# One exchange on ScalarE in a two-layer gated attention and expert kernel: a unit's exponentials and the copy of half of the next unit's values

## The chip, the cores and the metric

The kernel runs on one core of one Trainium2 chip. The metric is the device time of one execution in microseconds (us).

## What is computed

32 sequences of 128 tokens with 128 features pass through two layers. Each layer adds a cross attention over 77 context rows per sequence, scaled by tanh of a gate, and then a mixture of 8 experts of which each token takes 2, scaled by a second gate. Only the attention of layer 0 (8 heads of 64) is touched by the change. Cut to that:

```python
q = (x @ Wq).reshape(B, N, 8, 64).transpose(0, 2, 1, 3)        # x: layernormed
k = (context @ Wk).reshape(B, M, 8, 64).transpose(0, 2, 1, 3)
v = (context @ Wv).reshape(B, M, 8, 64).transpose(0, 2, 1, 3)
attn = jax.nn.softmax(jnp.einsum('bhnd,bhmd->bhnm', q, k) * scale, axis=-1)
out = jnp.einsum('bhnm,bhmd->bhnd', attn, v)
x = x + jnp.tanh(g_xattn[0]) * (out.transpose(0, 2, 1, 3).reshape(B, N, 512) @ Wo + bo)
```

## The kernel before

All engines walk the same list of units of work, the plan; each engine picks the kinds that concern it and issues its part in the order of the list. Waits are on semaphores only, so an engine that waits holds back everything behind it on that engine. `order()` writes the list out from four phases: layer 0's attention, layer 0's experts, layer 1's attention, layer 1's experts, each overlapping the next by a few steps. `attention0_steps` gives one step for each unit u, a unit being one sequence of 128 tokens with all 8 heads over its 77 keys (616 columns).

The query and key weights are multiplied into one matrix per head beforehand, and so are the value and output weights. Float32 products are made of three passes over a high and a low part. For unit u the pieces are:

- **score0** (PE, L840, six products into two banks): needs the normalised rows of the group of four sequences, their keys, and that DVE has subtracted the row maxima of unit u-1, since there is one pair of score banks. DVE then reduces the row maxima (L1265, row_max) and subtracts them (L1268, into prob).
- **exp0** (ACT, L1151): the exponentials, in place in prob. **divide0**: DVE sums the rows (L1319, row_sum) and takes the reciprocal (L1322); POOL multiplies (L1615).
- **turn0** (PE, L863, transposes in two sets, copied by ACT, L1171), one step later; **weigh0** (PE, L881, the product with the values in five chunks; DVE adds the gated result to x_res, L1328), two steps later.
- **v0** of unit u+1, in two halves of four heads (PE, L776 to L778, 77 x 512; copied by ACT, L1156, from bank to the tile vo). Both halves use one bank, so PE begins half 1 when ACT has copied half 0. SP sends each half out to DRAM (L690), and v0_load brings the rows back in the order of weigh0's chunks (L696, L697). ACT's copies of a unit wait until the halves of the unit before have landed in DRAM.

Between these lie the preparations for later groups, dealt out by u mod 4 in `prepare_attention0_at`: the key blocks of the next group (k0: PE L776 to L778 at 128 x 308; ACT copies the high part, L1113; DVE takes the difference as the low part, L1281), its norm, normalisation and transposition (xt). The bank of such a product is free again when DVE has taken the low part, and two banks alternate; one of them is the routing's too. `route_tasks` puts the routing of finished groups into the steps from unit 6 on (mturn L975, route L983 and L1378, pick L1396 to L1417, rank L999 and L1424, scatter L1687 on POOL).

`u` in the rows below: unit 16 is at about 141 to 145 us, unit 19 at 161 to 167, unit 21 at 174 to 180, unit 22 at 180 to 187.

Of the kernel before, what the change touches and what calls it, by code (L numbers as in the profile page):

```python
# [30 lines left out]
NSEQ, SEQ, D, NKEY = 32, 128, 128, 77  # L31
# [94 lines left out]
def attention0_steps(tasks):  # L126
    background = [("ctx", i) for i in range(2, CTX_SETS)] + [("weights1",), ("tables", 0)]
    background += [("expert", 0, e) for e in range(NEXP)] + [("tables", 1)]
    for u in range(NSEQ + 4):
        step = []  # L130
        more = prepare_attention0_at(u) if u < NSEQ else ([], [], [], [])
        if u < NSEQ:
            step += [("score0", u)] + more[0] + [("exp0", u)]
        if 0 <= u - 2 < NSEQ:
            step.append(("weigh0", u - 2))
        if u < NSEQ:
            step += [("v0_load", u)] + [("v0", u + 1, 0)][:u + 1 < NSEQ] + [("divide0", u)] + more[1]
        if 0 <= u - 1 < NSEQ:
            step.append(("turn0", u - 1))
        if u < NSEQ:  # L140
            step += [("v0", u + 1, 1)][:u + 1 < NSEQ] + [("bias0", u)] + more[2]
        step += more[3] + tasks.get(u, [])
        if background:
            step.append(background.pop(0))
        if u == NSEQ - 1:
            step += [("fetch", i) for i in range(AHEAD)]
        yield step
# [51 lines left out]
def prepare_attention0_at(u):  # L199

    g = (u + 1) // GS + 1 if u >= GS - 1 else 1
    if g >= NG:
        return [], [], [], []
    keys = ((3, 2, 1, 2) if g > 1 else (3, 3, 2, 0))
    turn = u % GS
    before = sum(keys[i] for i in ((3, 0, 1, 2) if g > 1 else (0, 1, 2))[:(turn + 1) % GS if g > 1 else turn])
    places = [[("k0", g, before + n)] for n in range(keys[turn])]
    if turn == 2:
        places.append([("xt", g)])
    places += [[]] * (3 - len(places))  # L210
    return places + [[("norm", g)] if turn == 0 else [("normalize", g)] if turn == 1 else []]
# [82 lines left out]
def order():  # L294

    first = prepare_attention0(0)
    out = [first[0], ("turn_weight", 0), ("turn_weight", 1), ("ctx", 0), ("wqk", 0), ("wqk", 1), ("turn_weight", 2)]
    out += first[1:] + [("wvo", 0), ("wvo", 1), ("ctx", 1), ("v0", 0, 0), ("v0", 0, 1), ("gates",)]
    tasks = [route_tasks(0, GS, 6, ((range(7), (5, 6, 7, 8)), (range(7), (5, 6, 7, 8)), ((0, 1, 2, 3, 3, 4, 5), (5, 5, 5, 5)))),
             route_tasks(1, 2 * GS, 13, (((0, 1, 3, 5, 6, 7, 9), (9, 11, 13, 15)), ((0, 1, 3, 5, 6, 7, 9), (8, 9, 10, 11)),  # L300
                                         ((0, 1, 2, 3, 4, 5, 6), (6, 6, 7, 7))))]
    after0 = [[("expert", 1, e)] for e in range(NEXP)] + first_keys_and_queries()
    phases = [(attention0_steps(tasks[0]), NSEQ), (expert_steps(0, tasks[0], NSEQ + 4, after0), LAYER_BLOCKS + 2),
              (attention1_steps(tasks[1]), U1 + 1), (expert_steps(1, tasks[1], U1 + 5, []), LAYER_BLOCKS)]
    begun = 0
    for i, (phase, alone) in enumerate(phases):
        after = phases[i + 1][0] if i + 1 < len(phases) else iter(())
        for _ in range(alone - begun):
            out += next(phase)
        begun = 0  # L310
        for step in phase:
            out += step
            out += next(after, [])
            begun += 1
        if i + 1 < len(phases):
            out += next(after)
            begun += 1
    out += [("spread", n) for n in ON_PE] + [("keep_busy",)] + [("load_last", q) for q in range(HT // 2)]
    out += [("combine_last", n) for n in range(HT)]
    apart = {t[1:] for t in out if t[0] == "rest"}  # L320
    return [u for t in out for u in ([t, ("rest",) + t] if t[0] in SPLIT_KINDS and t not in apart else [t])]
# [1402 lines left out]
```

## Time and profile before

| | |
|---|---|
| median of 3 runs | 786.98 us (784.69 to 788.65) |
| profiled execution | 788.87 us |
| its span in the trace | 787.1 us |
| mean granted TensorE clock | 0.928 of full speed |
| busy over the span | PE 85%, DVE 73%, POOL 60%, ACT 57% |

The span is what the profiler saw of one execution, from its first to its last instruction; what lies around it is 1.8 us here. Engines: PE is TensorE (PEld its weight loads), DVE VectorE, ACT ScalarE, POOL GpSimd, SP SyncE. Busy time is that of instructions, without waits. A granted clock of 1.00 is 2.4 GHz, of 0.50 it is 1.2 GHz, and a number between is the mean of a stretch with both.

### The profile page before, as it was taken

What the parts mean: (1) busy time and instruction counts of PE and PEld (TensorE: products, weight loads), DVE (VectorE), ACT (ScalarE), POOL (GpSimd) and SP (SyncE); (2) the same over time, 40 slices, a digit from 0 to 9 for tenths busy, and PEclk for the clock granted to TensorE, in tenths of its full rate; (3) what the DMA queues carried; (4) which work ended last, traced back from release to release, by engine and by line L of the source; (5) the groups of instructions that cost most, each with busy time, mean ns of one, the idle gap of its engine ahead of it and who ended that gap; (6) DMA issues with size and microseconds to landing.
All of it is one profiled execution on the core that took longest, in us unless ns stands there. A gap on an engine that the chain in (4) does not pass through costs nothing.

```text
span 787.1 us, 17248 instructions
## 1 busy us (share of the span) xinstructions
PE 672.4 (85%) x4720; PEld 609.5 (77%) x4720; DVE 574.3 (73%) x2005; ACT 448.7 (57%) x1219; POOL 475.7 (60%) x693
## 2 busy tenths in 40 slices
PE   6888988988887889988979898899888886878896
PEld 5667887877776889987878787788887886877796
DVE  3467877788667587999896888988878753845772
ACT  3466755665454555766666776676576543434451
POOL 4035346667457777787463344676566567677771
PEclk9999989998789799999998999999899986999998
DMA  9637546434344234545633534433534013344645
GB/s 263 176 82 191 161 136 172 120 112 128 102 113 131 86 102 115 151 117 143 174 87 90 118 90 90 129 100 76 119 93 99 24 43 96 107 120 122 188 132 178
DMA packets 130990, 95.91 MB, mean 122 GB/s; under 512 B 30504, under 2 KB 119112, under 8 KB 130832
## 3 DMA queue, kind: packets, MB, share of 16 engines
q1 hardware_dynamic: 113200, 69.15, 33.5%
q0 software_dynamic: 9088, 19.68, 7.7%
q10 hardware_dynamic: 8608, 5.99, 2.7%
q8 instruction: 40, 0.66, 0.4%
q14 instruction: 54, 0.44, 0.2%
HBM read 55.09 MB, written 44.10 MB: 126 GB/s over the span
## 4 chain that ended last, share of the span: by engine, by line
PE 40%; DVE 26%; issue 10%; ACT 9%; DMA 6%; POOL 5%; SPq 1%; DVEq 1%; ACTq 0%; POOLq 0%
PE banks L1032 9%; PE banks L896 4%; PE banks L1051 4%; DVE row_max L1265 4%; DMA y_rows<-y_sb,result_at 3%; DVE prob L1268 3%; PE banks L776 3%; PE banks L881 2%; PE banks L778 2%; PE banks L777 2%; PE banks L840 2%; POOL x_rows L1687 2%; ACT vo L1156 2%; POOL y_rows L1694 2%; PE banks L863 2%
## 5 line engine op out<-in xcount | busy, mean ns | idle before, releaser
L1694 POOL DMA_INDIRECT y_rows<-y_sb,result_at x156 | 151.0, 968 | 57.0 <-issue 30.2
L1032 PE MATMUL banks<-xb,up 128*128 128x128 f32 x936 | 143.5, 293 | 15.9 <-DVE hidden L1513 5.0
L1687 POOL DMA_INDIRECT x_rows<-xm,row x128 | 127.6, 997 | 36.0 <-issue 30.2
L1032 PEld LDWEIGHTS banks<-xb,up 128*128 128x128 f32 x936 | 125.9, 204 | 22.3 <-issue 10.1
L1051 PE MATMUL banks<-down,hidden 128*128 x624 | 100.4, 285 | 9.3 <-DVE y_sb L1530 8.7
L1649 POOL TENSOR_TENSOR v_flat<-v_raw,row_head 104x64 f32<-104x64 f32 (+1 forms) x128 | 55.7, 464 | 74.3 <-ACT v_raw L1187 73.9
L1051 PEld LDWEIGHTS banks<-down,hidden 128*128 128x128 f32 x624 | 85.5, 198 | 12.5 <-issue 12.1
L896 PE MATMUL banks<-v_flat,prob_t 128*128 128x108 f32 (+2 forms) x640 | 88.7, 288 | 3.2 <-issue 1.6
L896 PEld LDWEIGHTS banks<-v_flat,prob_t 128*128 128x128 f32 (+1 forms) x640 | 81.9, 202 | 11.0 <-ACT prob_t L1171 6.2
L1265 DVE TENSOR_REDUCE row_max<-banks 128x8 f32<-128x616 f32 x96 | 75.6, 787 | 20.4 <-PE banks L840 11.9
L1171 ACT ACTIVATE prob_t<-banks 128x512 f32<-128x512 f32 x192 | 72.6, 432 | 28.1 <-PE banks L863 26.2
L1615 POOL TENSOR_TENSOR prob<-prob,inv_sum 128x616 f32<-128x616 f32 x32 | 38.9, 1217 | 67.1 <-DVE inv_sum L1322 67.1
L1225 ACT ACTIVATE gate<-banks,block_bias 128x128 f32<-128x128 f32 x156 | 48.8, 364 | 45.0 <-PE banks L1032 40.5
L1505 DVE COPY up<-up 128x256 f32 x156 | 57.4, 368 | 11.0 <-issue 4.2
L1229 ACT ACTIVATE hidden<-banks 128x256 f32<-128x256 f32 x78 | 29.9, 384 | 60.1 <-PE banks L1032 56.4
L1268 DVE TENSOR_TENSOR prob<-banks,row_max 128x616 f32<-128x616 f32 x75 | 60.0, 800 | 2.6
L863 PE MATMUL banks<-ident,prob 128*128 128x128 f32 (+1 forms) x375 | 55.6, 281 | 0.0
L1513 DVE SCALAR_TENSOR_TENSOR hidden<-banks,block_bias,gate 128x128 f32<-128x128 f32 x156 | 46.9, 341 | 10.1 <-ACT gate L1225 9.1
L776 PE MATMUL banks<-wvo_h,ctx_th 128*77 128x512 f32 x64 | 31.5, 492 | 25.4 <-ACT vo L1156 25.2
L881 PE MATMUL banks<-vo_flat,prob_t 128*128 128x128 f32 (+1 forms) x320 | 47.2, 302 | 3.4 <-ACT prob_t L1171 3.4
L1530 DVE COPY y_sb<-banks 128x128 f32<-128x128 f32 x78 | 22.4, 288 | 35.8 <-DMA y_rows<-y_sb,result_at 23.6
L881 PEld LDWEIGHTS banks<-vo_flat,prob_t 128*128 128x128 f32 (+1 forms) x320 | 45.6, 218 | 3.4 <-ACT prob_t L1171 3.4
(212 smaller groups left out, 1619.8 us busy)
## 6 DMA issues: line engine op xcount, KB each, us to landing
v_rows<-vo SPq DMA_DIRECT2D x64, 154.0 KB
vo_flat<-v_rows SPq DMA_DIRECT2D x32, 256.0 KB
x_norm<-x_rows SPq DMA_DIRECT2D x86, 72.0 KB
x_far<-x_rows SPq DMA_DIRECT2D x70, 72.0 KB
gathered<-y_rows ACTq DMA_DIRECT2D x32, 128.0 KB
q_rows<-up_raw SPq DMA_DIRECT2D x8, 512.0 KB, 2.8
q_even<-q_rows SPq DMA_DIRECT2D x12, 256.0 KB
q_odd<-q_rows SPq DMA_DIRECT2D x12, 256.0 KB
```

Of the source, the lines that this page charges most:

```text
L863: done = pe.transpose(banks[0:chunk_rows[c], PT_BANK[k], c % 4 * SEQ:(c % 4 + 1) * SEQ], flat[:, c * P:c * P + chunk_rows[c]], ident[:, :])
L881: done = pe.matmul(banks[:, O_BANK, 0:D], prob_t[0:rows, b % 2, c, :], vo_flat[0:rows, b % 2, c, :], start=c == 0, stop=c == CHUNKS - 1)
L896: done = pe.matmul(banks[:, O_BANK, half * width:half * width + cols], prob_t[0:rows, u % 2, c, :], v1_flat[0:rows, first:first + cols], s ...
L1032: done = pe.matmul(banks[:, UP_BANK[i % 2], part * P:(part + 1) * P], block_w[:, i % WR, part // 2, part % 2 * P:(part % 2 + 1) * P], xb[: ...
L1051: done = pe.matmul(banks[:, Y_BANK[i % 2], 0:D], hidden[:, i % HR, half, :], of_expert(flat[:, (2 * layer + half) * D:], i, D), start=half ...
L1171: act.activation(dst, banks[0:rows, PT_BANK[k], 0:len(chunks) * SEQ], ACT.Copy).then_inc(sem("prob_t"))
L1265: dve.tensor_reduce(m_view, s_view, AX.X, ALU.max).then_inc(sem("row_max"))
L1268: dve.tensor_tensor(prob_view.rearrange("p (k s) n -> p k s n", k=2), s_view, m_view.unsqueeze(3).to_broadcast([P, 2, 4, NKEY]), ALU.subtr ...
L1505: dve.tensor_copy(block_w[:, i % WR, 1 - layer, :], src[:, bass.ds(at, HID1)]).then_inc(sem("block_w_dve"))
L1649: pool.tensor_tensor(v1_rows[0:rows, b % 2, half, chunks[0]:chunks[-1] + 1, :, 0:DK1], v1_raw[0:rows, chunks[0]:chunks[-1] + 1, half, :, : ...
L1687: pool.indirect_dma_start(out=x_rows[i // HG][:, :], out_offset=bass.IndirectOffsetOnAxis(ap=row[:, n, c:c + 1], axis=0), in_=xm[:, i % 2, ...
L1694: pool.indirect_dma_start(out=y_rows[k][:, :], out_offset=bass.IndirectOffsetOnAxis(ap=result_at[:, i % (2 * YR):i % (2 * YR) + 1], axis=0 ...
```

## The change

In each step of layer 0's attention the entry ("exp0", u) moves from before weigh0 to after ("v0", u + 1, 0). Only ACT does anything at exp0. It has nothing to do for weigh0 and v0_load, so on ACT the one effect is that exp0 of unit u comes after the copy of half 0 of unit u+1, and no longer before it. All other orders and all waits are as before.

```diff
@@ -130,11 +130,11 @@
         step = []
         more = prepare_attention0_at(u) if u < NSEQ else ([], [], [], [])
         if u < NSEQ:
-            step += [("score0", u)] + more[0] + [("exp0", u)]
+            step += [("score0", u)] + more[0]
         if 0 <= u - 2 < NSEQ:
             step.append(("weigh0", u - 2))
         if u < NSEQ:
-            step += [("v0_load", u)] + [("v0", u + 1, 0)][:u + 1 < NSEQ] + [("divide0", u)] + more[1]
+            step += [("v0_load", u)] + [("v0", u + 1, 0)][:u + 1 < NSEQ] + [("exp0", u), ("divide0", u)] + more[1]
         if 0 <= u - 1 < NSEQ:
             step.append(("turn0", u - 1))
         if u < NSEQ:
```

## Rows read from the trace of the kernel before

**Rows 1.** The page: busy time, share of the span and instructions of each engine.

```profile
PE 672.4 (85%) x4720; PEld 609.5 (77%) x4720; DVE 574.3 (73%) x2005; ACT 448.7 (57%) x1219; POOL 475.7 (60%) x693
```

**Rows 2.** Waits, 35 to 255 us: who waited for whom; us in total, times, longest.

```profile
ACT prob L1151 <- DVE prob L1268: 44.2, 27, 4.3
...
PE banks L776 <- ACT vo L1156: 24.6, 18, 3.0
...
DVE row_max L1265 <- PE banks L840: 11.9, 11, 4.0
DVE k_t L1281 <- ACT k_t L1113: 11.7, 15, 1.2
...
DVE rank_row L1424 <- PE banks L999: 5.0, 5, 1.4
...
ACT vo L1156 <- DMA v_rows<-vo: 3.9, 3, 2.8
...
DVE row_sum L1319 <- ACT prob L1151: 2.9, 6, 0.5
```

**Rows 3.** Timeline, unit 19: start us, us, engine line op out<-in xcount [idle before <-releaser].

```profile
161.42 0.40 PE L778 MATMUL banks<-wvo_l,ctx_th 128*77 128x512 f32 x1
...
162.80 0.80 DVE L1268 TENSOR_TENSOR prob<-banks,row_max 128x616 f32<-128x616 f32 x1
...
163.63 0.72 ACT L1151 ACTIVATE prob<-prob 128x616 f32<-128x616 f32 x1 [3.17 <-DVE prob L1268]
...
164.26 0.57 ACT L1156 ACTIVATE vo<-banks 77x512 f32<-77x512 f32 x1
...
164.88 0.46 PE L776 MATMUL banks<-wvo_h,ctx_th 128*77 128x512 f32 x1 [2.10 <-ACT vo L1156]
...
165.33 0.43 DVE L1281 TENSOR_TENSOR k_t<-banks,k_t 128x308 fp32r<-128x308 f32 x1
...
166.12 0.81 PE L840 MATMUL banks<-k_t,xt_h 128*128 128x308 f32 x4
166.30 0.19 DVE L1424 TENSOR_TENSOR rank_row<-banks,region 128x32 f32<-128x32 f32 x1 [0.54 <-PE banks L999]
```

**Rows 4.** Timeline, unit 21.

```profile
174.75 1.28 PE L881 MATMUL banks<-vo_flat,prob_t 128*128 128x128 f32 x10
...
175.36 0.80 DVE L1268 TENSOR_TENSOR prob<-banks,row_max 128x616 f32<-128x616 f32 x1
...
176.19 0.72 ACT L1151 ACTIVATE prob<-prob 128x616 f32<-128x616 f32 x1 [0.81 <-DVE prob L1268]
176.33 0.40 PE L778 MATMUL banks<-wvo_l,ctx_th 128*77 128x512 f32 x1
...
176.82 0.58 ACT L1156 ACTIVATE vo<-banks 77x512 f32<-77x512 f32 x1
...
176.95 0.80 DVE L1319 TENSOR_REDUCE row_sum<-prob 128x8 f32<-128x616 f32 x1
...
177.90 0.43 DVE L1281 TENSOR_TENSOR k_t<-banks,k_t 128x308 fp32r<-128x308 f32 x1
...
178.38 1.06 PE L983 MATMUL banks<-router,xm_t 128*128 128x8 f32 x8
```

**Rows 5.** Chain that ended last, unit 22: start us, us, what.

```profile
182.91 0.81 DVE row_sum L1319
...
188.40 0.81 DVE prob L1268
```

**Rows 6.** Timeline, unit 16.

```profile
141.83 2.01 PE L881 MATMUL banks<-vo_flat,prob_t 128*128 128x128 f32 x10
142.14 0.80 DVE L1268 TENSOR_TENSOR prob<-banks,row_max 128x616 f32<-128x616 f32 x1
...
144.15 0.40 PE L778 MATMUL banks<-wvo_l,ctx_th 128*77 128x512 f32 x1
```

**Rows 7.** Stretch 98 to 125 us: busy us (instructions), granted clock, DMA share, GB/s.

```profile
98.00:125.00 27.00, 23.71 (x145) 21.11 (x144) 20.71 (x74) 16.29 (x38) 12.74 (x18) 0.87 0.46 127
```

## The prediction

> **What bounds the kernel now.** I read the page's busy shares first: no engine is full over the span, PE 85%, DVE 73%, ACT 57% [rows 1]. The edit touches one stretch, layer 0's attention, about 35 to 255 us, so next come the waits of that stretch [rows 2]. Three rows decide. PE waits 24.6 us in 18 places for ACT's copy of the values (vo), nearly all of it before the second half of a unit's value product: both halves share one PSUM bank, so PE cannot write half 1 until ACT has copied half 0. ACT itself waits 44.2 us for DVE's subtraction before the exponentials. DVE waits little. So ACT is not short of time; it is short of order: it stands at the exponentials of unit u while the finished half 0 of unit u+1 lies behind them.
>
> The stretch is no single bound. It goes by fours, since the next group's keys, its norm, and the routing of an earlier group are dealt over u mod 4. The timelines of units 19 (u mod 4 = 3) and 21 (u mod 4 = 1) and the chain through unit 22 (u mod 4 = 2) show who is late.
> Unit 19 [rows 3]: half 0 is complete at 161.82 (161.42 + 0.40), the subtraction only at 163.60; the exponentials run 163.63 to 164.35, the copy starts at 164.26, and PE stands 2.10 us. DVE is late here.
> Unit 21 [rows 4]: the subtraction ends at 176.16, half 0 at 176.73. PE is late here, and ACT's exponentials fill just the gap; PE waits for nothing. Behind them on DVE lie the row sums (176.95), the reciprocal and the low half of a key block (177.90 to 178.33), and the router's product, which needs that block's bank, starts at 178.38.
> Unit 22 [rows 5]: the chain that ended last runs on DVE without a break from the row sums through the routing of a group to the next unit's subtraction (189.21).
>
> **The change, part by part.** Nothing is added or removed. On ACT, the exponentials of unit u (32 of them, 0.72 us [rows 3]) change places with the copy of half 0 of unit u+1 (0.57 to 0.58 us); 31 units have such a copy. PE, POOL and SP keep their orders; DVE too. The copy no longer waits for the subtraction; the exponentials now wait for half 0's product too, and for the copy's other wait, that the transfers of the previous unit's values out of that tile have landed. Behind the exponentials on ACT are the next key block's high half, the copies of the turned probabilities, and half 1's copy; who waits for them is DVE (row sums first), then PE and POOL.
>
> *Where DVE is late (u mod 4 = 3, and units 1, 2, 5, 25).* The copy moves from 164.26 to about 161.86, and PE's 2.10 us go. But the next scores also need the subtraction: PE may start them at 163.65 at the earliest, 2.5 before the 166.12 of [rows 3]. What comes next is DVE: after the subtraction its own work (low key block, residual, row sums, reciprocal, low key block) lasts to 165.76 as before, and what goes is its wait for the rank products, 0.54 us here. Over the stretch those waits are 5.0 us in 5 places [rows 2]; with 1.6 us of the 11.9 that row_max waits for PE (those in the same units) DVE gets at most 6.6 us back. So of PE's 24.6 us most turn into a wait for the scores' bank, which DVE's subtraction frees. Unit 25, where PE's wait is longest (3.0), gives 1.5: DVE has block tables to build there and the key copies before it are late too. Units 1 and 2 give 1.1: DVE waits there for ACT's high halves (that row of [rows 2]), and those come earlier only by the one copy of 0.57 that was passed. Unit 29 gives 0.5.
>
> *Where PE is late (17 units).* In unit 21 the copy would start at 176.77 instead of 176.82: it gains 0.05. The exponentials start 0.50 after it (0.59 less the 0.09 by which neighbours on ACT overlap, as 176.91 against 176.82), at 177.27 and not 176.19: 1.08 later. Row sums start at 178.01 and not 176.95, the low key block ends at 179.39 and the router's product starts 1.06 later, the scores behind it too. I give this full 1.06 to units 10, 13, 14, 21, 22 and 26: 6.4 us. In u mod 4 = 2 it is DVE's chain of [rows 5] that moves. In units 9, 17, 18 and 30 half 0 and the subtraction end together (within 0.15), so the exponentials lose only the copy: four times 0.59 less a little behind PE, 2.2. In units 3 to 8 DVE has little routing yet and part of row_max's 11.9 us of waits [rows 2] lies there; about a third of six times 1.06 stays: 2.4. Sum of losses 11.0.
>
> *Where PE is late because its clock is low (units 12, 16, 28).* The granted clock is 0.87 from 98 to 125 us [rows 7]; ten products of weigh0 take 2.01 us in unit 16 [rows 6], at the 1.2 GHz level, against 1.28 in unit 21 [rows 4]. Half 0 ends at 144.55, 1.61 after the subtraction (142.94). Here PE's earlier start from the unit before (about 2.5, as in unit 19) brings half 0 to about the subtraction, so the delay shrinks to the copy, and PE, which is behind everything, keeps what DVE cannot use: 2.6 us in the three. Behind units 20 and 24 ACT has four normalisations in line and gives 0.7 back.
>
> Sum: gains 6.6 + 1.5 + 1.1 + 0.5 + 2.6 - 0.7 = 11.6; losses 11.0; net 0.6 us sooner. Against the profiled execution's own 788.87 that is 788.3; its median of three is 786.98, so I say 786.4.
> After the stretch nothing changes but its offset: the experts and layer 1 start as early as this stretch ends.
>
> *Bounds.* The gain cannot exceed PE's removed waits, 24.6 us; nothing else gets shorter. The loss, if every late unit's 1.08 stayed and no wait came back, is 17 x 1.08 = 18.4. I take neither end: the scores need both PE's bank and DVE's subtraction, so each side limits the other.
>
> The Trainium skill (Perfetto Trace Analysis, Optimization Strategy) says to find the gaps of the most-contended engine and to make what they wait for come sooner. Followed here, with PE as that engine by its weight loads (77% of the span), the rule makes the time 24.6 us less; the row for DVE shows 5.0 of use to it. It is rival A below.
>
> **The rivals.**
> A, *PE's waits really go* (faster). For it: 18 waits, 24.6 us, and in the half-speed spells PE is behind all else. Against it: scores wait for the subtraction. If DVE keeps 6.6 and PE half of the remaining 18.0 while a third of the losses stay hidden behind PE, it is 6.6 + 9.0 - 7.3 = 8.3 less: 778.7. It decides when units with u mod 4 = 0 start at least 1 us earlier after their predecessor. By that rule of the skill it would be this mechanism in full, 762.4.
> B, *exponentials stand behind a copy whose product is late* (slower). DVE's row sums start 1.06 later in the 17 units and the chain of [rows 5] pays, while in u mod 4 = 3 only DVE's 5.0 come back: 11.0 - 5.0 = 6.0 more, 793.0. It decides when u mod 4 = 0 gives nothing back, as at full clock it might.
> C, *a transfer takes the wait's place*: ACT's copy waited 3.9 us in 3 places for values on their way out, once 2.8 [rows 2]; the exponentials now wait behind it. With the 1.2 us that the exchange itself costs in each, they come about 2 to 4 us late there, some 8 in all; 2.7 are in the sum above; with all on the chain it is 5.3 more than the forecast, 791.7.
> D, *the order does not matter*, because DVE binds throughout: 787.0.
>
> **How the numbers follow.** A measurement of this kernel tells a difference of 0.5%, 3.9 us, from none. The forecast (786.4) gets 0.40 and D 0.05, both within 0.5%; A 0.26; B 0.20; C 0.09. The forecast's own range is 783 to 790.5, since each of its two sums of 11 may be off by a quarter. For 8 in 10 the range goes to A's 778.7 less a little and B's 793.0 and more: 778 to 794. Faster by over 0.5%: 0.27; within: 0.45; slower: 0.28, of which all but little is B and C.
>
> **What would show it.** Right, if PE's wait for vo falls from 24.6 to under 5, if PE instead waits for DVE's subtraction (prob) before scores (none now), if DVE's wait for ACT's exponentials rises from under 3 to 15 or more, and rank_row's wait for PE falls from 5.0 to about 1. In a unit like 21 the row sums should follow the subtraction by about 1.85 us, not 0.79; in one like 19 the scores should follow it at once. The stretch from unit 0's row_max to unit 31's should be as long as now within 2 us. It is wrong if that stretch shrinks by over 4 (DVE had more slack than I gave it) or grows by over 4 (nothing is given back), or if PE's low-clock spells become fewer or more: at 1.2 GHz a unit's weigh0 costs 2.01 and not 1.28 us [rows 4, 6].

## The result, and the profile after

The changed kernel takes 792.01 us (median of 8 executions, 789.27 to 794.4), the kernel before 787.51 on the same chip (8 executions, 784.06 to 789.84): a ratio of 1.0076 with a 95% interval of 1.0052 to 1.0100, slower by about 6.0 us (4 to 8). Ratios, here and below, are those on record over fast executions alone and not the quotients of the medians; the two medians here are 4.5 us apart. The forecast was 786.4, no difference that can be told. The profiled execution has a span of 790.0 us, against 787.1.

The page of the kernel after, busy time and then the chain that ended last:

```profile
PE 667.2 (84%) x4720; PEld 600.9 (76%) x4720; DVE 578.5 (73%) x2005; ACT 445.2 (56%) x1219; POOL 475.5 (60%) x693
...
PE 33%; DVE 30%; issue 12%; ACT 11%; POOL 7%; DMA 4%; DVEq 1%; SPq 1%; POOLq 0%; ACTq 0%
```

The instruction counts are those of [rows 1]; PE's busy time is even 5.2 us less. On the whole span nothing points at the loss. So go to the stretch. From unit 0's row_max to unit 31's it lasts 218.29 us (35.64 to 253.93) and lasted 213.04 (35.55 to 248.59): 5.25 us more, in layer 0's attention. Behind it the changed kernel's span is 2.4 us shorter; the granted TensorE clock of the next 146 us was 0.97 there and 0.93 before. So the spans differ by only 2.9. The waits of the kernel after in this attention, 35 to 262 us (who waited for whom; us in total, times, longest):

```profile
DVE row_sum L1319 <- ACT prob L1151: 29.7, 26, 3.4
...
ACT vo L1156 <- PE banks L778: 25.0, 18, 3.0
...
ACT vo L1156 <- DMA v_rows<-vo: 18.3, 9, 3.0
ACT prob L1151 <- DVE prob L1268: 16.1, 9, 5.2
...
PE banks L996 <- DVE k_t L1281: 8.7, 4, 3.1
PE banks L776 <- ACT vo L1156: 8.3, 11, 2.6
DVE row_max L1265 <- PE banks L840: 8.0, 7, 4.0
ACT x_norm L1134 <- DVE shift_n L1307: 6.7, 7, 1.1
...
DVE rank_row L1424 <- PE banks L999: 2.8, 2, 1.4
...
PE banks L840 <- DVE prob L1268: 0.7, 1, 0.7
```

Against [rows 2] the reader sees both sides of the exchange. ACT's wait for the subtraction fell from 44.2 to 16.1 and PE's for vo from 24.6 to 8.3, 16.3 us that PE no longer stands there. In exchange DVE stands 29.7 us before its row sums (2.9 before), and there is a row that was not there at all: PE waits 8.7 us in 4 places to begin the rank products (L996), for DVE's low key block. ACT's normalisation waits 6.7 us for an instruction of DVE on four elements (shift_n), where it waited 1.3.

Where the 5.25 us lie: the step from one row_max to the next, after minus before, summed by the unit it starts from (worked out from the timelines of both). The forecast's column sorts the prediction's own terms by unit, with units 1 and 2 sharing their 1.1 and units 3 to 8 losing 0.4 each. The last column is a second trace of the changed kernel (the third group's, below) against the same trace of the kernel before; it shows how far single traces vary.

| step starts at | forecast | measured | second trace |
|---|---|---|---|
| u mod 4 = 1 | +1.1 | +1.6 | +1.1 |
| u mod 4 = 2 | +5.2 | +5.2 | +3.6 |
| u mod 4 = 3 | -5.8 | -0.4 | -0.4 |
| u mod 4 = 0 | -1.1 | -1.1 | -0.8 |

In three rows the sum came near the forecast; the gain in u mod 4 = 3 did not come in either trace.

**Where PE is late.** Timeline of the kernel after, units 21 and 22 (start us, us, engine line op, what [idle before <-releaser]); to be read beside [rows 4, 5]:

```profile
181.21 0.59 ACT L1156 ACTIVATE vo<-banks 77x512 f32<-77x512 f32 x1 [1.39 <-PE banks L778]
...
181.71 0.71 ACT L1151 ACTIVATE prob<-prob 128x616 f32<-128x616 f32 x1
...
182.45 0.79 DVE L1319 TENSOR_REDUCE row_sum<-prob 128x8 f32<-128x616 f32 x1 [1.20 <-ACT prob L1151]
...
183.39 0.42 DVE L1281 TENSOR_TENSOR k_t<-banks,k_t 128x308 fp32r<-128x308 f32 x1
183.56 1.22 POOL L1615 TENSOR_TENSOR prob<-prob,inv_sum 128x616 f32<-128x616 f32 x1 [0.57 <-DVE inv_sum L1322]
183.74 1.06 DVE L1307 SCALAR_TENSOR_TENSOR shift_n<-mean_var,rstd 128x4 f32<-128x4 f32 x1
183.87 1.06 PE L983 MATMUL banks<-router,xm_t 128*128 128x8 f32 x8 [1.03 <-DVE k_t L1281]
...
184.83 1.65 ACT L1134 ACTIVATE x_norm<-x_res,shift_n,rstd 128x128 f32<-128x128 f32 x4 [0.98 <-DVE shift_n L1307]
...
185.93 0.80 DVE L1265 TENSOR_REDUCE row_max<-banks 128x8 f32<-128x616 f32 x1
186.77 0.80 DVE L1268 TENSOR_TENSOR prob<-banks,row_max 128x616 f32<-128x616 f32 x1
...
188.66 0.71 ACT L1151 ACTIVATE prob<-prob 128x616 f32<-128x616 f32 x1
189.40 0.80 DVE L1319 TENSOR_REDUCE row_sum<-prob 128x8 f32<-128x616 f32 x1 [1.19 <-ACT prob L1151]
...
194.09 0.77 DVE L1265 TENSOR_REDUCE row_max<-banks 128x8 f32<-128x616 f32 x1
```

The exponentials start 0.50 behind the copy, as worked out, and DVE stands 1.20 us before the row sums. The router's product (L983) starts 4.90 us behind unit 21's row_max (178.97) and started 3.85 behind it before (174.53): 1.05 later, the forecast 1.06. In unit 22 the row sums follow the subtraction by 189.40 - (186.77 + 0.80) = 1.83 us, and did by 182.91 - (181.33 + 0.80) = 0.78 before. The whole step 22 is 8.16 us long (185.93 to 194.09) and was 7.09 (180.51 to 187.60): 1.07 more, the forecast 1.06. DVE, which carries the chain there, had the same work and stood still.

**Where DVE is late.** Timeline of the kernel after, unit 15:

```profile
135.42 0.59 ACT L1156 ACTIVATE vo<-banks 77x512 f32<-77x512 f32 x1 [1.82 <-DMA v_rows<-vo]
...
136.94 0.80 DVE L1268 TENSOR_TENSOR prob<-banks,row_max 128x616 f32<-128x616 f32 x1
...
137.78 0.72 ACT L1151 ACTIVATE prob<-prob 128x616 f32<-128x616 f32 x1 [1.76 <-DVE prob L1268]
...
138.53 0.79 DVE L1319 TENSOR_REDUCE row_sum<-prob 128x8 f32<-128x616 f32 x1
...
139.47 0.43 DVE L1281 TENSOR_TENSOR k_t<-banks,k_t 128x308 fp32r<-128x308 f32 x1
...
140.05 0.36 PE L996 MATMUL banks<-picked,earlier 128*128 128x32 f32 x1 [3.06 <-DVE k_t L1281]
...
141.11 1.38 PE L840 MATMUL banks<-k_t,xt_h 128*128 128x308 f32 x4
141.29 0.19 DVE L1424 TENSOR_TENSOR rank_row<-banks,region 128x32 f32<-128x32 f32 x1 [1.39 <-PE banks L999]
```

The copy is early now (135.42, before the subtraction) and PE has finished half 1 at 137.00. But its next work, the rank products, writes the bank in which the last key block lies, and DVE takes that block's low half only behind the row sums, at 139.47. PE stands 3.06 us, and the scores, in line behind the rank products, come at 141.11 and not at the subtraction's end, 137.74. The wait that was removed stands one instruction further on. The kernel before had the same limit without showing it: there the rank products start at 139.09, 3.11 us behind the subtraction's start (135.98), and 140.05 is 3.11 behind 136.94. The copy came earlier and the rank products did not. DVE waits 1.39 us for the rank where it waited 0.88, since the products themselves took longer: PE stood from 137.00, and its granted clock was 0.65 from 139 to 140 and 0.50 from 140 on (0.97 and then 0.50 in the kernel before). Unit 23 is the same case with a step of 7.65 us in both. The transfer for which the copy waited 1.82 costs nothing: ACT stands another 1.76 us before the exponentials.

Unit 19 lacks that limit: its rank products wait for a block that DVE takes ahead of the row sums. The kernel after:

```profile
167.91 0.25 PE L996 MATMUL banks<-picked,earlier 128*128 128x32 f32 x1 [1.31 <-DVE k_t L1281]
...
169.27 1.22 POOL L1615 TENSOR_TENSOR prob<-prob,inv_sum 128x616 f32<-128x616 f32 x1 [0.93 <-DVE inv_sum L1322]
169.45 0.18 DVE L1424 TENSOR_TENSOR rank_row<-banks,region 128x32 f32<-128x32 f32 x1
169.67 0.91 DVE L1427 TENSOR_TENSOR rank_hot<-hot,rank_row 128x64 f32<-128x64 f32 x1
...
170.61 0.22 DVE L1430 TENSOR_REDUCE row_f<-rank_hot 128x8 f32<-128x64 f32 x1
```

and the kernel before:

```profile
166.52 0.27 DVE L1427 TENSOR_TENSOR rank_hot<-hot,rank_row 128x64 f32<-128x64 f32 x1
...
166.83 0.22 DVE L1430 TENSOR_REDUCE row_f<-rank_hot 128x8 f32<-128x64 f32 x1
```

Here the wait for the rank (0.54 us) did go, and DVE came to rank_hot 0.63 us earlier in the step. But there POOL's division is in its first half, and rank_hot lasted to just behind its end, 0.91 us and not 0.27. The next instruction, row_f, starts 4.83 us behind the row_max (165.78, and 162.00 before) in both kernels, and the step is 5.25 us in both.

### The profile page after: what moved, and what is told of

Same layout as the page of the kernel before. It is cut to its first block, busy times and chain, and to the rows that moved or that the text cites. A ratio compares the mean times of both kernels' runs of the same rounds, so it can differ in the third digit from the quotient of the medians.

```text
span 790.0 us, 17248 instructions
## 1 busy us (share of the span) xinstructions
PE 667.2 (84%) x4720; PEld 600.9 (76%) x4720; DVE 578.5 (73%) x2005; ACT 445.2 (56%) x1219; POOL 475.5 (60%) x693
## 4 chain that ended last, share of the span: by engine, by line
PE 33%; DVE 30%; issue 12%; ACT 11%; POOL 7%; DMA 4%; DVEq 1%; SPq 1%; POOLq 0%; ACTq 0%
PE banks L1032 6%; PE banks L896 4%; DVE row_max L1265 4%; POOL x_rows L1687 3%; PE banks L881 3%; PE banks L1051 3%; PE banks L776 3%; DMA y_rows<-y_sb,result_at 2%; DVE prob L1268 2%; ACT prob L1151 2%; POOL y_rows L1694 2%; PE banks L840 2%; DVE row_sum L1319 2%; DVE x_res L1537 2%; PE banks L778 2%
## 5 line engine op out<-in xcount | busy, mean ns | idle before, releaser
L1032 PE MATMUL banks<-xb,up 128*128 128x128 f32 x936 | 141.1, 289 | 18.7 <-DVE hidden L1513 7.2
L1032 PEld LDWEIGHTS banks<-xb,up 128*128 128x128 f32 x936 | 122.6, 200 | 26.3 <-issue 9.5
L1051 PE MATMUL banks<-down,hidden 128*128 x624 | 98.8, 282 | 8.3 <-DVE y_sb L1530 8.2
L1051 PEld LDWEIGHTS banks<-down,hidden 128*128 128x128 f32 x624 | 83.8, 195 | 11.7 <-issue 10.9
L896 PE MATMUL banks<-v_flat,prob_t 128*128 128x108 f32 (+2 forms) x640 | 86.8, 285 | 3.1 <-issue 1.6
L1505 DVE COPY up<-up 128x256 f32 x156 | 59.3, 380 | 11.5 <-issue 4.0
L1156 ACT ACTIVATE vo<-banks 77x512 f32<-77x512 f32 x64 | 38.0, 594 | 46.0 <-PE banks L778 27.6
L1319 DVE TENSOR_REDUCE row_sum<-prob 128x8 f32<-128x616 f32 x32 | 25.4, 795 | 30.6 <-ACT prob L1151 29.7
```

Source lines behind the costliest of these rows:

```text
L896: done = pe.matmul(banks[:, O_BANK, half * width:half * width + cols], prob_t[0:rows, u % 2, c, :], v1_flat[0:rows, first:first + cols], s ...
L1032: done = pe.matmul(banks[:, UP_BANK[i % 2], part * P:(part + 1) * P], block_w[:, i % WR, part // 2, part % 2 * P:(part % 2 + 1) * P], xb[: ...
L1051: done = pe.matmul(banks[:, Y_BANK[i % 2], 0:D], hidden[:, i % HR, half, :], of_expert(flat[:, (2 * layer + half) * D:], i, D), start=half ...
L1505: dve.tensor_copy(block_w[:, i % WR, 1 - layer, :], src[:, bass.ds(at, HID1)]).then_inc(sem("block_w_dve"))
```

## The experiments

The theory from these rows: the loss is DVE's idle time before the row sums where PE is late, above all in u mod 4 = 2 (forecast's losses, rival B); the gain is missing because a bank is freed late and because a small DVE instruction now starts inside POOL's division. When the groups were planned, that instruction was taken to be shift_n, which lies in u mod 4 = 1, and not rank_hot. Rivals: the exponentials now wait for transfers (C), or the order there matters little and something else moved. The exponentials' place can be chosen for each unit, so the change splits by units. All kernels of the second to fourth group, the kernel before too, took some 60 us more on those occasions, nearly all of it behind this attention, for a reason that isn't known; ratios are only taken inside a group.

**First group: the exchange in a quarter of the units.** Before 787.48 us. The condition takes the values `u % GS == 1`, `2`, `3` and `0` (GS is 4). Cuts inside a line are written as three dots here and below:

```diff
-            step += [("score0", u)] + more[0] + [("exp0", u)]
+            step += [("score0", u)] + more[0] + [("exp0", u)] * (not (u % GS == 1))
...
-            step += ... + [("divide0", u)] + more[1]
+            step += ... + [("exp0", u)] * (u % GS == 1) + [("divide0", u)] + more[1]
```

> The exchange only in the units with u mod 4 = 1 (8 of 32). Theory 'row sums late' (the loss comes from the exponentials standing behind a copy whose product is late, 1.06 us a unit, and DVE's and PE's chains pay): units 9, 13, 17 and 21 cost 0.4 to 1.4 us each, unit 25 gives some back, so 0 to 4 us slower than before, 2 likeliest. Theory 'transfers' (the loss comes from the three to nine places where the copy, and now the exponentials behind it, wait for values on their way out): none of those places has u mod 4 = 1, so no change.

> The exchange only in the units with u mod 4 = 2. 'Row sums late': in the trace of the changed kernel the steps behind these units took 5.2 us more in sum, so 4 to 6 us slower than before, nearly the whole of the change's loss. 'Transfers': only units 6 and 14 wait for one, at most 2 us slower.

> The exchange only in the units with u mod 4 = 3, where DVE is late. The prediction's step gave 6.6 us back here. Theory 'bank': the rank products now wait for the bank that DVE's low key block frees, 3.06 us in units 15 and 23 of the changed kernel, so little of it comes back: 0 to 2 us faster. If the step was right and only undone by the others, 5 to 7 us faster. 'Transfers': no change.

> The exchange only in the units with u mod 4 = 0. 'Row sums late': without the advance from the units before, exponentials wait for half 0 1.1 to 2.5 us longer, but DVE has slack here: 0 to 3 us slower. 'Transfers': unit 8 only, at most 1 us slower.

| exchange in | median us | ratio to before (95%) |
|---|---|---|
| u mod 4 = 1 | 786.94 | 1.0005 (0.9979 to 1.0030) |
| u mod 4 = 2 | 796.21 | 1.0096 (1.0061 to 1.0131) |
| u mod 4 = 3 | 786.54 | 0.9983 (0.9950 to 1.0016) |
| u mod 4 = 0 | 788.73 | 1.0007 (0.9975 to 1.0040) |

One quarter alone loses 7.6 us, as much as the whole change or more (the intervals overlap), and the other three cannot be told from nothing. In the trace of the second kernel the steps that start at u mod 4 = 2 are 4.2 us longer and the ones behind them 2.4. The exchange in u mod 4 = 3 alone, where I had forecast the gain, gives nothing; its row of waits shows the same new wait as the full change, which the kernel before does not have:

```profile
PE banks L996 <- DVE k_t L1281: 4.5, 4, 2.1
```

**Second group: what stops the gain.** Before 851.08 us. Two repairs, each on the changed kernel and, as a control, on the kernel before. The shift: DVE issues shift_n for the next group at exp0's place in u mod 4 = 1, ahead of the row sums, where POOL is not yet dividing:

```diff
-                elif kind == "normalize":
-                    n = t[1]
+                elif kind == "exp0" and t[1] % GS == 1 and t[1] > GS and (t[1] + 1) // GS + 1 < NG or kind == "normalize" and not 2 <= t[1] < NG:
+                    n = (t[1] + 1) // GS + 1 if kind == "exp0" else t[1]
```

The bank: the rank products take, of the two banks in which key blocks alternate, the one that is freed first:

```diff
+    rank_banks = {t: SPLIT_BANK for k, t in enumerate(plan) if t[:2] == ("rank", 0) and t[2] < NG - 2 and place[[s for s in plan[:k] if s in place][-1]] % 2}
...
-            return ROUTE_BANK if t[1] == 0 else SPLIT_BANK if of_experts(t) else V_BANK
+            return rank_banks.get(t, ROUTE_BANK) if t[1] == 0 else SPLIT_BANK if of_experts(t) else V_BANK
```

> The changed kernel, with DVE's shift_n (four elements per partition, for the next group's normalisation) of units 5 to 25 moved ahead of the row sums in the units with u mod 4 = 1, where DVE waits for the exponentials anyway. In the changed kernel it took 1.05 to 1.23 us in all of these units, since POOL's division of the probabilities ran at the same time, against 0.15 in units 13, 17 and 21 before. Theory 'collision' (part of the loss is DVE held up by POOL's division): 2 to 3 us faster than the changed kernel, so 2 to 4 slower than before. Theory 'row sums late' alone: the 0.9 us lie on slack and nothing changes, 5 to 6 slower than before.

> The kernel before, with the same shift_n moved in the same way; control. 'Collision': only units 5, 9 and 25 had 1.05 us there before, so 0 to 2 us faster. 'Row sums late' alone: no change.

> The changed kernel, with the rank products in whichever of the two key-block banks was freed earlier, so that they no longer wait 3.06 us for the low key block in units 15 and 23. Theory 'bank': PE reaches the next scores up to 2 us earlier in these two, DVE's rank work too: 2 to 4 us faster than the changed kernel, so 2 to 4 slower than before. If the bank is not what keeps the predicted gain away: as the changed kernel, 5 to 6 slower than before.

> The kernel before with the same banks for the rank products; control. There the rank products came after half 1, which came after the key block's bank was free, and waited for no bank: both theories say no change.

| kernel | median us | ratio to before (95%) |
|---|---|---|
| after + shift | 854.05 | 1.0037 (1.0010 to 1.0065) |
| before + shift | 851.49 | 1.0012 (0.9988 to 1.0037) |
| after + bank | 852.94 | 1.0029 (1.0001 to 1.0058) |
| before + bank | 849.03 | 0.9977 (0.9957 to 0.9998) |

The changed kernel without repair stands at 1.0076 (and 1.0080 in the next group), so each repair takes about 0.4 to 0.5% off it, with an uncertainty of some 0.4% since it comes from two groups. On the kernel before, the shift does nothing that can be told and the bank gives 0.23%. So the times alone don't show that the bank is worth more with the exchange than without. The bank's effect in the trace, unit 15 of after + bank, beside the 3.06 us above:

```profile
135.31 0.59 ACT L1156 ACTIVATE vo<-banks 77x512 f32<-77x512 f32 x1 [3.33 <-issue]
...
136.13 0.72 ACT L1151 ACTIVATE prob<-prob 128x616 f32<-128x616 f32 x1 [0.23 <-DVE prob L1268]
...
136.71 0.18 PE L996 MATMUL banks<-picked,earlier 128*128 128x32 f32 x1
...
137.19 0.81 PE L840 MATMUL banks<-k_t,xt_h 128*128 128x308 f32 x4
...
138.17 0.18 DVE L1424 TENSOR_TENSOR rank_row<-banks,region 128x32 f32<-128x32 f32 x1
...
138.39 0.90 DVE L1427 TENSOR_TENSOR rank_hot<-hot,rank_row 128x64 f32<-128x64 f32 x1
```

The rank products go without a wait, the scores start 1.09 us after the subtraction (136.10) and not 3.37 as in the kernel after, and DVE no longer waits before rank_row. The steps 15 and 23 become 0.9 and 0.8 us shorter than before; with the change alone they were 0.8 longer and equal. But this is not the exchange's gain: in before + bank, without the exchange, the same two steps are shorter by the same 0.9 and 0.8 (unit 15: 5.26 us, and 5.25 with the exchange). There DVE still waits 0.54 us before rank_row, and then rank_hot is short:

```profile
138.05 0.19 DVE L1424 TENSOR_TENSOR rank_row<-banks,region 128x32 f32<-128x32 f32 x1 [0.54 <-PE banks L999]
...
138.27 0.28 DVE L1427 TENSOR_TENSOR rank_hot<-hot,rank_row 128x64 f32<-128x64 f32 x1
```

With the bank free, unit 15 is like unit 19: the exchange takes the 0.54 away, and POOL's division gives it back (0.90 for 0.28).

**Third group: the empty wait, and the parts together.** Before 846.88 us. The changed kernel again; the changed kernel with the routing's pick ahead of the row sums on DVE in u mod 4 = 2, so that DVE has about 2 us of work where it waits for the exponentials; the exchange in all units but u mod 4 = 2; and the changed kernel with pick, shift and bank.

```diff
+        early = [t for t in tasks.get(u, []) if t[0] == "pick" and u < NSEQ]
...
-            step += ... + [("exp0", u), ("divide0", u)] + more[1]
+            step += ... + [("exp0", u)] + early + [("divide0", u)] + more[1]
...
-        step += more[3] + tasks.get(u, [])
+        step += more[3] + [t for t in tasks.get(u, []) if t not in early]
```

> The changed kernel again, on the chip of the other three, as their measure: 4 to 8 us slower than before.

> The changed kernel, with the routing's pick (some 2.1 us of small DVE operations in the units with u mod 4 = 2 from unit 6 on, which need nothing of the exponentials) put on DVE ahead of the row sums. Theory 'row sums late': the loss in these units is DVE standing idle until the late exponentials end while its own work is the chain; filled with the pick, the idle time is no loss, and 4 to 5 of the lost us come back: 0 to 3 us slower than before. If the loss in these units has another cause (clock spells, transfers, POOL): as the changed kernel.

> The exchange in all units but those with u mod 4 = 2. 'Row sums late', with 7.6 us for those alone and about 6 for all: the other 24 units give 0 to 3 us back, so 3 us faster to 1 slower than before. If the exchange costs in all units alike: 3 to 5 us slower.

> The changed kernel with all three repairs: pick and shift_n ahead of the row sums and the rank products in the bank that is free first. If the three found causes are the whole loss and the step that gives PE's waits back was right apart from them, 2 to 8 us faster than before; if something else costs, no faster than before.

| kernel | median us | ratio to before (95%) |
|---|---|---|
| after, again | 853.74 | 1.0080 (1.0049 to 1.0112) |
| after + pick | 841.75 | 0.9962 (0.9939 to 0.9985) |
| exchange but in u mod 4 = 2 | 847.58 | 1.0017 (0.9993 to 1.0042) |
| after + pick, shift, bank | 835.37 | 0.9867 (0.9827 to 0.9907) |

Leaving out the one quarter takes 0.6 of the 0.8% away. Moving the pick into its wait takes 1.2% away, more than the loss; the fourth group shows how much of that is the pick's own. Unit 22 of after + pick:

```profile
180.81 0.80 DVE L1268 TENSOR_TENSOR prob<-banks,row_max 128x616 f32<-128x616 f32 x1
...
182.17 0.08 DVE L1396 MATCH_VALUE_LOAD top_idx<-top_val,ranked 128x8 f32 x1
...
182.71 0.70 ACT L1151 ACTIVATE prob<-prob 128x616 f32<-128x616 f32 x1
...
183.98 0.19 DVE L1417 TENSOR_TENSOR counts<-counts,group_sum 128x8 fp32r<-128x8 f32 x1
184.09 0.78 DVE L1319 TENSOR_REDUCE row_sum<-prob 128x8 f32<-128x616 f32 x1
...
186.64 0.77 DVE L1265 TENSOR_REDUCE row_max<-banks 128x8 f32<-128x616 f32 x1
```

The pick runs from 182.17 to 184.17, over the exponentials, and DVE stands before nothing. The step is 186.64 - 179.97 = 6.67 us against 8.16 after and 7.09 before. The row sums themselves come 2.48 after the subtraction, later than in the kernel after; it is DVE's idle time that cost, not the row sums' date. The control is before + pick (fourth group), where the same step takes 6.66 us: with the wait filled, the exchange costs nothing in this unit.

**Fourth group: whose gain is it.** Before 849.42 us. The pick could be worth something without any exchange. So: the kernel before with the pick ahead; the kernel before with all three repairs; the exchange only from unit 9 on (`u > 8`), for the transfers of the first units, behind which the exponentials come late; and the repaired kernel with the exchange in u mod 4 = 3 alone.

> The kernel before, with the pick ahead of the row sums in the same units as in c1_after_pick. In this order DVE does not wait for the exponentials there, so there is no idle time to fill. If the 10 us of c1_after_pick came from the filled wait: no change, within 2 us. If the pick's place is worth something by itself: 4 us faster or more.

> The kernel before, with all three repairs of c3_after_all. The two smaller ones were +0.12% and -0.23% alone. If the exchange is what the repairs set free: 0 to 3 us faster, so 8 or more slower than c3_after_all's 11.3. If the repairs carry it alone: 8 us faster or more.

> The exchange in units 9 to 31 only. Theory 'transfers': the waits of the copy for values on their way out in units 4, 5, 6 and 8 of the changed kernel, 1.7 to 3.0 us with late exponentials behind them, are a large part of the loss: 3 us or more of the 6 to 7 come back. 'Row sums late': the trace shows the first nine units as a whole 0.5 us earlier with the exchange than without: 5 to 8 us slower than before.

> All three repairs, and the exchange only in the units with u mod 4 = 3. If what the repairs set free is the advance in these units, where DVE is late: as c3_after_all, 9 to 13 us faster than before. If the units 1, 2, 25 and 29 and those at the low clock matter as much: 3 to 8 faster.

| kernel | median us | ratio to before (95%) |
|---|---|---|
| before + pick | 844.22 | 0.9931 (0.9900 to 0.9962) |
| before + pick, shift, bank | 843.97 | 0.9925 (0.9899 to 0.9952) |
| exchange from unit 9 on | 858.35 | 1.0099 (1.0059 to 1.0138) |
| before + all three, exchange in u mod 4 = 3 | 842.98 | 0.9933 (0.9900 to 0.9965) |

I had expected nothing of the pick alone: it is worth 5.9 us by itself. In its trace the steps that start at u mod 4 = 2 are shorter by 5.7 us in all, while the other steps sum to 2.5 shorter, about as much as single traces vary. Why an earlier pick helps a kernel in which DVE waits little before the row sums I have not taken apart. The exchange from unit 9 on is no better than the whole change, so the first nine units, with their transfers, lose nothing. In u mod 4 = 3 alone the exchange adds nothing to the repaired kernel (0.9933 against 0.9925 without it); the 5.7 us by which it beats the kernel before are the repairs' own. So the bank was not all that kept the gain of this class away.

## Why the prediction was wrong

**The loss held, as a mechanism and about in size.** Of the units given "full 1.06", unit 22's step grew by 1.07 and unit 21's router product came 1.05 later; the six steps (10, 13, 14, 21, 22, 26) grew by 0.7 to 1.9, in sum 7.6 for 6.4. DVE's wait before the row sums rose to 29.7 us ("15 or more"). Row sums follow the subtraction by 1.84 in unit 21, as the forecast 1.85. The first and third groups show that u mod 4 = 2 carries it: alone +0.96%, left out +0.17%. Filled with other work the kernel stands at -0.38%; corrected by what the pick is worth by itself (-0.69%), filling the wait took back 1.18 - 0.69 = 0.5%, with an uncertainty as large, since the numbers come from two groups. The step of unit 22 (6.67 against 6.66 us) says it more sharply.

That the class sums came so near has luck in it. In u mod 4 = 1 shift_n grew by 0.9 to 1.1 us in units 13, 17 and 21, because it now starts inside POOL's division, and no term of the forecast had that. The shift kernel's steps of this class are 3.8 us shorter in sum than the changed kernel's (single traces), and on the kernel before the same shift changes none of them by over 0.03. The second trace has 3.6 and not 5.2 in u mod 4 = 2. The forecast's own count is loose as well: it speaks of 17 late units and lists 16, has units 3, 5 and 7 both among the late and where DVE is late, and puts 2.4 for a third of six times 1.06, which is 2.1.

**The step that failed** is the largest gain, 6.6 us where DVE is late: DVE's "own work ... lasts to 165.76 as before, and what goes is its wait for the rank products". Measured for the class: 0.4 us. Two things stood in its place.

In units 11, 19 and 27 the wait went (1.31, 0.54 and 0.87 us, 2.7 in sum), but DVE's work did not last as before. It came to rank_hot while POOL's division ran, and rank_hot grew by 0.67, 0.64 and 1.01 us, 2.3 in sum. Only units 11 and 27, where DVE had also waited for the scores, became shorter, by 1.6 and 0.6. The division starts behind the row sums and the reciprocal, which the exchange doesn't make earlier there. That this is the limit is read from the traces: row_f starts 4.83 us behind the row_max in unit 19 with and without the exchange, and in after + pick, where rank_hot comes just ahead of the division (0.23 us), the next one (L1432, row) takes 0.87 for 0.17 and the step is again 5.26. No kernel with POOL's division in another place was run.

In units 15 and 23 the wait did not even go (2.3 us in the two before, 2.8 after). The prediction let PE go on as soon as the subtraction was done, and the row that was to prove it (PE waits for DVE's prob before the scores) reads 0.7 us in 1 place. Between half 1 and the scores stand the rank products, and they need a bank that DVE's low key block frees behind the row sums; they start 3.1 us behind the subtraction's start with or without the exchange. In the kernel before half 1 ended just then, so this wait was hidden behind PE's wait for vo. Freeing the bank shortens both steps by 0.9 and 0.8, but as much on the kernel before, so this was not the exchange's to gain. So rank_row's wait fell from 5.0 to 2.8 in all, not to 1. The prediction moved instructions in time and asked for each only what it waited for before, not what it would meet.

**The other terms.** PE's wait for vo fell to 8.3, not under 5. The class u mod 4 = 0 gave back its 1.1; of the 2.6 for units 12, 16 and 28 came 1.5 and 1.2 in two, and unit 16 lost 0.9. Unit 25 gave 2.1 for 1.5. The stretch grew by 5.25 (3.5 in the second trace): by the prediction's own sign "nothing is given back". The TensorE clock did not turn it: over layer 0's attention its mean was 0.92 in both kernels. It did change behind it, and "nothing changes but its offset" was off by the 2.4 us above.

**The rivals.** B's mechanism, exponentials behind a copy whose product is late, is the one that lost the time, and its 6.0 us are what was lost. But its sum is right by errors that cancel: it credits 5.0 to u mod 4 = 3 (0.4 measured), and it gives nothing for u mod 4 = 0 and the other gains, of which 1.1 came in u mod 4 = 0. C (transfers) is not borne out: ACT's copy waits 18.3 us for them, not 3.9, but as in unit 15 ACT would have stood before the exponentials anyway, leaving the first nine units out changes nothing for the better, and the exchange in u mod 4 = 3 alone, in whose trace the copy waits 12.3 us for transfers in 5 places, loses nothing (0.9983). A (PE's waits really go) is refuted: 16.3 of 24.6 us of them went, and the time rose. The Trainium skill (Perfetto Trace Analysis, Optimization Strategy) says to look for the gaps of the most-contended engine, within the stretch of interest, and to make what they wait for come sooner. Followed with PE as that engine throughout, this gave 762.4, and 792.0 was measured. Here two engines alternate in being late from unit to unit, and the engine with the largest share of the span was not the one to follow.

**What stays open.** With all three repairs the exchange looks useful: 0.9867 with it and 0.9925 without, 0.58% apart with an uncertainty of about 0.5% (0.40 and 0.27 combined), from two groups. That is barely more than nothing, and the two weren't run side by side. Why the pick alone is worth 0.69% was only found, not explained. The best version is the changed kernel with pick, shift and bank: 1.33% faster than the kernel before (0.93 to 1.73%), some 11 us of 846.88.

## What to carry to other kernels

Exchanging two instructions that wait for different engines can help where the first one's input is late and costs where the other's is, so in a loop that changes its bottleneck from turn to turn, cost it turn by turn and place it turn by turn. A wait that is removed gives its time only if the next instruction on that engine has all it needs: ask for each what frees its bank or buffer, not only what it was seen waiting for, since that wait may have been hidden behind the one removed. A wait removed on one engine can also push its next work into another engine's way: look at what runs at the new time. Where an exchange leaves the chain's engine idle for a microsecond, independent work of that engine in the gap takes the cost away (6.67 against 6.66 us in unit 22). Measure the moved work on the old kernel too: here it was worth 0.69% there, more than half of what it seemed to bring.

## What the runs showed of the hardware

A DVE instruction on four elements of each partition takes 0.15 us, and took over 1 us where it started early inside POOL's division. All instances of shift_n between 35 and 255 us (duration ns min/median/max), before:

```profile
L1307 DVE SCALAR_TENSOR_TENSOR shift_n<-mean_var,rstd x7: 152/153/1059, 47.6 to 209.3; 128x4 f32<-128x4 f32 x7
```

after:

```profile
L1307 DVE SCALAR_TENSOR_TENSOR shift_n<-mean_var,rstd x7: 194/1056/1227, 46.6 to 216.0; 128x4 f32<-128x4 f32 x7
```

and with the shift kernel's earlier place:

```profile
L1307 DVE SCALAR_TENSOR_TENSOR shift_n<-mean_var,rstd x7: 149/150/191, 46.7 to 212.1; 128x4 f32<-128x4 f32 x7
```

In unit 21 above, POOL's division starts at 183.56 and ends at 184.78; shift_n starts at 183.74 and ends at 184.80. In unit 19 rank_hot (L1427, 128x64, two inputs) does the same and takes 0.91 us, where it takes 0.27 in the kernel before. Just ahead of it rank_row (L1424), which also has two inputs but one of them in a PSUM bank, starts inside the same division and takes 0.18, no longer than the 0.19 before. The Trainium skill (SBUF — State Buffer, Who interferes with whom, and Summary: rules for kernel authors) says that a DVE instruction with two inputs in SBUF contends with a GpSimd instruction that reads SBUF, and that the second one to issue is blocked until the first finishes; the trace agrees, with 1.06 us for an instruction of 0.15.
